# Constant products of TensorE in the second attention and in the preparation of the third: 56 more for each batch item

## The reference, cut to what matters

```
for layer in 0..3:
    xn = layernorm(x)
    s = attention_l(xn)        # layer 1: 16 heads of 8, causal, then Wo
    g = silu(ffn_l(xn))        # layer 1: gate and up products, both operands and
                               #   weights rounded to FP4 in blocks of 16, then down
    x = x + s * g
# layer 2's attention has an RMS norm with weights ahead of its q, k, v products
```

## Time and profile before

| | |
|---|---|
| median of 3 runs | 4678.98 us (4678.09 to 4681.33) |
| the profiled execution | 4681.39 us, its span 4679.6 us |
| PE busy | 3769.4 us (81%), x20191 |
| DVE busy | 2666.6 us (57%) |
| ACT busy | 1891.5 us (40%) |
| TensorE clock granted, mean | 0.924 of full |

### The profile page before, as it was taken

One profiled execution on the slowest core, in us unless ns is written; L12 is line 12 of the kernel. 1 busy time (PEld: TensorE's weight loads), 2 busy tenths in 40 slices (PEclk: granted clock), 3 DMA queues, 4 the chain that ended last, 5 costly groups with the idle time before them and its releaser, 6 DMA issues. The chain is left out here.

```text
span 4679.6 us, 57461 instructions
## 1 busy us (share of the span) xinstructions
PE 3769.4 (81%) x20191; PEld 1899.0 (41%) x20355; DVE 2666.6 (57%) x5719; ACT 1891.5 (40%) x3814; POOL 782.5 (17%) x715
## 2 busy tenths in 40 slices
PE   5878888788887888887887888877888787887776
PEld 2344433435334443344433444343533444334434
DVE  5565556555566545664556555655556654566455
ACT  2443444343433434343344433444343343434324
POOL 0031101220012300222003120032101230012213
PEclk9989998999989999899998999899998999989987
DMA  4000010000000001000100001000000000100030
GB/s 139 28 8 22 5 34 28 15 14 11 28 28 28 1 18 36 20 22 1 39 28 8 22 5 34 28 9 21 11 28 28 28 1 16 36 23 22 1 81 19
DMA packets 79876, 113.86 MB, mean 24 GB/s; under 512 B 11452, under 2 KB 60167, under 8 KB 79047
## 3 DMA queue, kind: packets, MB, share of 16 engines
q1 hardware_dynamic: 73662, 101.08, 7.0%
q10 hardware_dynamic: 5898, 8.77, 0.6%
HBM read 80.68 MB, written 28.34 MB: 23 GB/s over the span
## 5 line engine op out<-in xcount | busy, mean ns | idle before, releaser
L704 DVE TENSOR_REDUCE nmax<-banks 128x1 f32<-128x512 f32 (+3 forms) x1216 | 761.1, 658 | 376.1 <-PE banks L543 208.9
L634 ACT ACTIVATE probs<-banks 128x512 f32<-128x512 f32 (+3 forms) x1536 | 673.7, 491 | 493.1 <-PE banks L561 489.9
L93 PE MATMUL banks<-filler,identb 128*128 128x512 bf16 x2384 | 689.3, 413 | 106.3 <-PEq L73 60.5
L543 PE MATMUL banks<-ks,qs 72*128 72x512 bf16 (+3 forms) x1536 | 472.0, 348 | 100.2 <-DVE nmax L704 70.2
L561 PE MATMUL banks<-qs,ks 74*128 74x512 bf16 (+3 forms) x1536 | 488.8, 352 | 39.9 <-ACT probs L634 21.5
L93 PEld LDWEIGHTS banks<-filler,identb 128*128 128x128 bf16 x2536 | 267.9, 107 | 412.2 <-issue 219.5
L599 PE MATMUL banks<-probs,v 128*32 128x512 f32 (+3 forms) x3072 | 352.9, 533 | 54.9 <-DVE att L691 33.4
L671 POOL TENSOR_SCALAR_AFFINE_SELECT probs<-probs 128x512 f32<-128x512 f32 x256 | 206.8, 809 | 1124.1 <-ACT probs L634 1124.1
L543 PEld LDWEIGHTS banks<-ks,qs 72*128 72x128 bf16 x1536 | 142.0, 101 | 427.9 <-DVE nmax L704 280.0
L333 POOL TENSOR_TENSOR rstd<-var,neghalf 128x4 f32<-128x4 f32 x24 | 24.3, 1011 | 1522.0 <-DVE var L261 1522.0
L561 PEld LDWEIGHTS banks<-qs,ks 74*128 74x128 bf16 x1536 | 144.4, 103 | 291.9 <-ACT probs L634 120.5
(11 more groups left out here) (410 smaller groups left out, 6065.8 us busy)
## 6 DMA issues: line engine op xcount, KB each, us to landing
qs<-parts_scratch SPq DMA_DIRECT2D x288, 96.0 KB
ks<-parts_scratch SPq DMA_DIRECT2D x288, 96.0 KB
parts_scratch<-parts SPq DMA_DIRECT2D x48, 384.0 KB, 2.8
qs<-max_parts SPq DMA_DIRECT2D x192, 4.0 KB
x<-in_x SPq DMA_DIRECT2D x9, 256.0 KB, 2.8
w_up_s<-in_w_up ACTq DMA_DIRECT2D x1, 2048.0 KB
x_scratch<-x SPq DMA_DIRECT2D x8, 256.0 KB, 3.7
factor_scratch<-att SPq DMA_DIRECT2D x8, 256.0 KB
```

Of the source, the lines that this page charges most:

```text
L93: nc.tensor.matmul(K.ps[:, bank, :], K.identb[:, :], K.filler[:, :], start=True, stop=True)
L543: mm = nc.tensor.matmul(K.ps[:, b, i * keys:(i + 1) * keys], K.qs[0:72, 4 * g + j, t * P:(t + 1) * P], K.ks[0:72, 4 * g + j, 0:keys], star ...
L634: nc.scalar.activation(probs[:, 4 * (q % QUADS) + m % 4, q0:T], K.ps[:, bank("second", m), q0:T], ACT.Exp, scale=scale).then_inc(exped, 1)
L704: nc.vector.tensor_reduce(nmax[:, t, h:h + len(heads)], K.ps[:, n % 2, 0:len(heads) * keys].rearrange("p (j k) -> p j k", k=keys), AX.X, A ...
```

## The change

`attention` gets an argument `waits_first`, 10 in the second attention and 0 in the other two, whose code stays as it was. With it, the second attention issues 10 products ahead of the feed-forward's first transposes, two instead of one after the first of a step's first scores (steps 1 to 11, 11 more), 3 behind the turn back of a group if second scores follow (steps 23, 31, 39), and 2 ahead of the weighings q = 10 to 14 and 10 ahead of q = 15. In the third preparation 9 become 12, and 3 more stand behind the last transposes. That is 50 and 6 for each item, 448 in all. Nothing is removed.

```
                 if rms:
-                    keep_busy(nc, K, 3, 9)
+                    keep_busy(nc, K, 3, 12)
                     for t in range(NT):
                         pe.wait_ge(xr_ready, t + 1)
                         nc.tensor.transpose(K.ps[:, 7, t * P:(t + 1) * P], K.xr[:, t, :],
                                             K.ident[:, :]).then_inc(xr_turned, 1)
+                    keep_busy(nc, K, 3, 3)
                     pe.wait_ge(xrT_ready, 1)
...
+                keep_busy(nc, K, 5, waits_first)
                 beside.run(beside.on_tensor, -1)
                 for s in range(STEPS):
...
                         mm.then_inc(oturned, 1)
+                        if waits_first and second:
+                            bank_read("second", second[0])
+                            keep_busy(nc, K, bank("second", second[0]), 3)
...
                             if causal and s < LAG:
-                                keep_busy(nc, K, 3, 1)
+                                keep_busy(nc, K, 3, 2 if waits_first and n == first[0] and s else 1)
...
                     for q in weigh:
                         g, k = divmod(q, NT)
+                        if waits_first and s > 8 * NG + 1:
+                            keep_busy(nc, K, 0, 10 if q == 4 * NG - 1 else 2)
...
-                attention(nc, K, True, K.w1_o, beside=ffn)
+                attention(nc, K, True, K.w1_o, beside=ffn, waits_first=10)
```

More of the change, by code:

```diff
@@ L472, in run_alone, with attention @@
     K.clear()
-def attention(nc, K, causal, wo=None, bo=None, combine=True, beside=None, after_store=False):
+def attention(nc, K, causal, wo=None, bo=None, combine=True, beside=None, after_store=False,
+              waits_first=0):
     (scored, reduced, turned, hi_ready, lo_ready, masked, rows, scored2, exped, weighed, oT_ready, oturned, vec,
```

## The result

The changed kernel took 4653.9 us, the median of six runs (4642.47 to 4663.11), against 4679.0 us for the kernel before, timed beside it (six runs, 4678.09 to 4685.02): a ratio of 0.9943, with an interval of 0.9925 to 0.9961. That is 25 us less, 18 to 35 by the interval; 4651 us was predicted. The profiled execution took 4646.16 us, 7.7 us under that median.

A forecast was written before the change was run, and what follows sets the result against it. The second attention was read as running about 38 of 96 us at half clock, costly only where others wait for TensorE. Terms summed to -3.8 us an item, -30 for eight, from 4681.4 to 4651 us; range 4627 to 4684.

The forecast's parts named there:

- tail: Second attention from q = 12: half clock goes, but products ahead of the last weighings cost; mean +0.7 us an item.
- steps 12 to 16: Second attention, first second score to second turn of maxima: doubled products keep full clock; -2.1 us an item.
- steps 25 to q = 12: Second attention: products behind step 31's turn back run free and may restore the clock sooner; -0.5 us an item.
- rest: All of an item that the change doesn't touch: no term in the forecast, so 0.
- head, with steps 1 to 8: Start of the second attention: ten products keep full clock, first scores begin sooner; -1.4 us an item, -2.0 to -0.3.
- to the first second score: Second attention, behind the head up to step 12: no term of its own, counted in the head's -1.4 us.
- step 23: A turn back in the second attention: three products on TensorE's path, less a little slack; +0.5 us an item.
- third preparation: Added products fill its waits, so five of eight items lose their half clock; mean -1.0 us an item.
- rival A: Clock falls anyway in the second attention's first two pauses; head -0.3, steps 12 to 16 0; 4677 us; chance 0.18.
- Rival B: Tail decides: half clock behind q = 12 stays, +2.7 us there, kernel slower at 4700 us; chance 0.12.

The follow-up runs named there:

- e1_single_first: The changed kernel with one product instead of two after a step's first scores (steps 1 to 11): 4673.0 us, ratio 0.9973 to the kernel before.
- e4_no_head: The changed kernel without the ten products ahead of the second attention's first transposes: 4661.0 us, ratio 0.9942 to the kernel before.
- e2_no_tail: The changed kernel without the products ahead of weighings q = 13, 14 and 15: 4626.9 us, ratio 0.9875 to the kernel before.

## Why the prediction was right, and where it was not

The time was right, 4651 against 4653.9, and so was the mechanism in the main: nothing but the clock pays, and the tail gives some back. But that the terms came to -3.8 us is partly luck. One was wrong in sign, by 2.1 us with the stretch behind it, and what made up for it came out better by 0.5 to 0.9 us each than I had it, or was taken as unchanged: steps 12 to 16, steps 25 to q = 12, and the rest. The code outside the loop gave 0.5 us an item on top, which the table leaves out. And the trace that the right column is read from is 7.7 us below the median.

| term, us per item | predicted | measured |
|---|---|---|
| head, with steps 1 to 8 | -1.4 | +0.86 |
| to the first second score | (in the above) | -0.2 |
| steps 12 to 16 | -2.1 | -3.0 |
| step 23 | +0.5 | +0.5 |
| steps 25 to q = 12 | -0.5 | -1.1 |
| tail | +0.7 | +0.6 |
| third preparation | -1.0 | -1.04 |
| rest | 0 | -0.5 |

**Head: the step that failed.** "I take the clock to stay full" held for the gate and up pairs only. A gate and up pair now takes 0.70 us from L862 to L864 and the L862 row is 0.86 us long, against 1.54 before, so that much came. The first scores started 7.16 us behind the transposes on the mean, 8.13 before: 1.0 of the 1.3 us counted. What is late next is the transfer, as predicted, too: 2.04 us of wait put down to it. But I charged that wait with one stretch of 3.4 us at half clock at the most and took the middle between the ends; the rows show 6.8 us: in five of eight items it begins about this wait, in items two and three already at the waits of the pairs. Then the first scores, the mask product and the doubled products run at 0.50 on the path that DVE waits for, and from the first scores to the first turn of maxima it is 12.69 us instead of 10.86. Only the fifth item came out as the prediction had it, 17.20 us. The seven products through this wait removed the half clock in all eight items, and shortened the head by 1.9 us; so the cause is shown and not only argued. It is what rival A said of the first pause, and in this one place A was right; but its price, -0.3, was too good as well, against +0.7 with the stretch to the first second score.

The Trainium skill, TensorE: Matmul & The Clock Gate, Part 4 (PE-mode transpose), which says that a transpose does not count as busy the same way as another product, was named for that rival. In the fourth item's rows the clock is 1.00 from the transposes through both pairs and falls only behind them, so the fall at the wait for the transfer does not need that rule; no run here isolates it.

**Steps 12 to 16: right in cause, too small.** I compared with the next group's 6.38 us, which has twelve more products in it. The same 34 products need 4.94 us at full clock, in seven of eight items. Undoing the doubled products alone put 8.1 us back. They are no guarantee, as the counts above show.

**Step 23** cost the 0.5 us reckoned, and taking its products away gave it back. **Steps 25 to 33** gained 0.9 and the stretch to q = 12 0.2, more than the 0.5 taken, which went by one wait of DVE. The half-clock stretch there, which I called nearly free, fell from 13.7 us to 6.8 in the fourth item. Whether the products of step 31 did that is not shown: no run takes them away alone.

**Tail.** The price was right: q = 15 came 1.5 us later behind q = 12 where 1.4 was said, and the clock is full there. The steps of my working fit less well: it gives 1.8 us at q = 15 and not 1.4, and with 0.3 of slack and 0.35 for the scores taken off that is 1.15 and not 1.0, with the 0.35 counted twice. By item, five paid 1.1 us (from 13.3 to 14.45) where 1.0 was said, and three gained 0.2 (from 14.7) where I had +0.2. The ten cost 1.79 us at the output product, 2.13 less 0.34 of slack. They ran in the order of the program, as the Trainium skill, TensorE: Matmul & The Clock Gate, Part 3, has it; the trace agrees, with the weighing q = 15 at 1924.01, behind the ten that start at 1921.75. Rival B's price was never reached, as its condition, half clock behind q = 12, did not occur.

**Third preparation.** 13.24 us in all items. The three behind L353 suffice; the other three are not needed for it.

**The rest** I took to be unchanged, and for the change it nearly is. That is luck of the combination: across these kernels the same untouched code takes from 444.1 to 449.1 us an item, 40 us over the eight, more than the whole effect. It is TensorE's pauses and the clock in other places. The six products alone gain 18 us there, which is why six products of 56 are worth as much as all. Some 13 of these 18 us are the half-clock stretch behind the third preparation, which falls where it costs nothing; in e1_single_first and e4_no_head, which have the two longest rests of the table, it falls late in all eight items. Why it falls early or late, and the other 5 us, stay open.

## What to carry to other kernels

Constant products keep the clock only if they reach the wait in which it is lost, the wait for a transfer included; here, filling the first pause moved the half clock to a later one, and filling the last and longest one as well kept it. They belong where TensorE waits, and cost up to their full 0.21 us each where others wait for it (ahead of the last weighings, behind the turn of step 23): count the slack behind a product before placing it. And judge such edits stage by stage over all passes of the loop, the untouched stages too: here totals of parts did not add up (28 and 22 us alone, 25 together), since an edit also moved the half clock inside blocks that it does not touch, while the edited stages nearly did.

## What the runs showed of the hardware that was not expected

Whole items do not take any length. In the changed kernel they took 549.6, 553 and 556 us (552.8, 553.0, 556.4, 553.1, 549.6, 553.1 and 556.0 from one to the next), before mostly 556 and otherwise 560 and 563; the steps are about 3.4 us, as long as the shortest half-clock stretch in the rows. It is a tendency and no more: in e2_no_tail two items took 552.0 and 554.0 us. If it holds, a small edit may seem to bring nothing, or 3.4 us an item at once, 27 us for the eight; no run here was made to show that.

Where the clock is lost in the head was decided in one wait. With 1.34, 0.69 and 1.11 us of idle time left as they were, seven products in the 2.04 us wait for the transfers, beside the ten, kept the clock in every item's head; the ten ahead of the transposes, which cut a pause of 3.95 to 1.34 us, kept it in one of eight. And half clock in the head did not cost the later steps: with the ten taken away the head was at half clock in all eight items and steps 12 to 16 at full clock, 4.93 us, in all eight.

The same 3.4 us at half clock cost next to nothing or 1.6 us, by where they fell. Over all traces here, the block behind the third preparation took 30.8 us in the items in which they began 13 to 15 us into it, 30.72 in the one item without any half clock, and 32.2 to 32.4 us, but for one item of 31.5, where they began at 25 to 26 us.
